# Three-step warm-up of a fused attention and channel-mix kernel: half projections, weight transposes and the order of step 2 moved

## The chip, the cores and the metric

The kernel runs on one core of one Trainium2 chip, with one launch. The metric is the device time in microseconds (us) of that launch. Before the change it was 272.54 us, the median of three runs (272.11 to 272.74).

## The reference, cut to what matters

The input x has 4 sequences of 1024 tokens with 256 channels, all in float32. Two sublayers run one after the other:

```python
def _L0_attn_ref(x, ...):            # called with layernorm(x)
    q = x @ Wq + bq                  # 16 heads of 16
    k = (x @ Wk + bk) @ Wc @ We      # 4 key/value heads of 16
    v = (x @ Wv + bv) @ Wc @ We
    qf, kf = elu(q) + 1, elu(k) + 1
    num = einsum(qf, cumsum(kf v^T)) # causal linear attention along the tokens
    den = einsum(qf, cumsum(kf)) + 1e-6
    y = x + (num / den) @ Wo + bo
    return layernorm(y) * gamma + beta

def _L0_ffn_ref(x, ...):             # called with layernorm(x)
    x_prev = x shifted by one token, zero first
    xr = mu_r * x + (1 - mu_r) * x_prev
    xk = mu_k * x + (1 - mu_k) * x_prev
    return sigmoid(xr @ W_r.T) * (relu(xk @ W_k.T)**2 @ W_v.T)

x = x + _L0_attn_ref(layernorm(x), ...)
x = x + _L0_ffn_ref(layernorm(x), ...)
```

## The kernel before, in words

The tokens are cut into 8 chunks of 128; a chunk is 128 tokens of all 4 sequences, so its tiles are 128x1024 or 2x128x512. Each engine has its own instruction list, written out by hand; semaphores tie them together, and an engine stops at the first wait that is not met, whatever stands behind it. `step(c)` (c = 0 to 6) works on up to four chunks at once: the front (transposes, keys, values, queries) of chunk n = c+1, the attention of chunk c (scores, mask, outputs, division), the output projection and the norms of chunk m = c-1, and the channel mix of chunk f = c-2. So steps 0 and 1 have no channel mix; step 2 is the first with all four. `finale` drains the last ones.

The parts that the change and the prediction touch:

- TensorE. `out_projection(m, i, bank)` (L520) is half i of chunk m's projection, 8 matmuls. `ffn_weight(i, bank)` (L601) turns one of the three FFN weights with 4 transposes. `keep_busy` (L597) issues matmuls whose results nobody reads. `scores(c, b)` (L482), `outputs(c, b)` (L500), `denominators(n)` (L465, waits for `prod`), `mix_r`, `mix_k`, `mix_v_parts` as named. `step` (L607), `first_full_step` (L644) and `middle_of_step` (L658) give the order.
- VectorE (DVE). `mask` (L1142), `divide` (L1154), `add_residual` (L1165: the sum of projection and residual, then row statistics), `norm_x` (L1068), `token_shift` (L1201), `centre` (L1175), `states` and `key_sums` (L1121, L1115), `second_residual` (L1186), `reciprocal` (L1128, L1130).
- ScalarE (ACT). Copies out of PSUM (L828), exponentials of the queries (L848, L850), `normalise_x` (L894), `normalise_y` (L900), `normalise_z` (L910).
- GpSimd (POOL). `add_bo` (L269), `add_beta` (L276), `denominator_terms` (L284, writes `prod`), `token_difference` (L292, writes `dz`), `first_norm`, `second_norm` and `norm_x` (L227 to L237), `finish` (L299). In steps from 2 on, POOL's list is: token difference, norm of x, `add_bo(n)`, `first_norm(m)`, `add_beta(n)`, `denominator_terms(n)`, `second_norm(m)`, `finish(f)`. `add_beta(n)` overwrites a buffer of which there are two, so it begins with this wait, and `prod` stands behind it:

```python
if n >= 2:
    pool.wait_ge(s_x2, 4 * n - 4)      # all four rows of second_residual(n - 2)
```

The PSUM banks are x0, x1, x2 (one each), ps_y (outputs) and z0 to z3 (scores, reciprocals).

## Time and profile before

| | |
|---|---|
| median of 3 runs | 272.54 us (272.11 to 272.74) |
| the profiled execution's own time | 272.06 us |
| its span in the profile | 270.3 us |
| PE busy | 258.1 us (95%) |
| DVE busy | 233.2 us (86%) |
| ACT busy | 168.8 us (62%) |
| POOL busy | 149.0 us (55%) |
| granted TensorE clock | 1.00 |

All times in the rows below are of the profiled execution, counted from the start of its span; 1.8 us of its own time lie outside the span. A row gives start and duration; the duration of a pipelined group is a little longer than the distance to the next one. An item in brackets behind a row is the idle time ahead of it and what ended it.

### The profile page before, as it was taken

Reading aid. Unit: us, or ns where it says so; the run is one execution under the profiler, and the core shown is the slowest. Engines: PE = TensorE matmul, PEld = TensorE weight load, DVE = VectorE, ACT = ScalarE, POOL = GpSimd, SP = SyncE. Lnnn points to the kernel's source line nnn. Section 1 sums busy time; section 2 is a strip of 40 time slices with the busy share of each in tenths; the row PEclk is TensorE's granted clock in tenths of the full one; section 3 lists DMA queues with packets and bytes.
Section 4 is the critical chain, followed back from the end, with each engine's and each line's share of the span. In section 5 each row is a group of like instructions: output and inputs, shape, how many; then the busy total and the mean of one; then the engine's idle time right before and its main releaser. Section 6 shows DMA issues by size and latency. Waiting matters only on the chain.

```text
span 270.3 us, 7775 instructions
## 1 busy us (share of the span) xinstructions
PE 258.1 (95%) x3047; PEld 195.4 (72%) x3047; DVE 233.2 (86%) x562; ACT 168.8 (62%) x339; POOL 149.0 (55%) x171
## 2 busy tenths in 40 slices
PE   7998989999998999999999999999999999999893
PEld 6867657877874788759875888758875877686663
DVE  6677779889799899998999899996999868999694
ACT  2579786794667856586648765686348730357570
POOL 3567484579944695366833685366433533173542
PEclk9999999999999999999999999999999999999999
DMA  6910320000200040002200020002000020000213
GB/s 180 266 67 4 79 80 2 4 2 0 81 2 0 2 158 0 2 4 76 82 2 0 2 81 1 2 4 78 2 0 4 2 80 2 0 0 0 80 42 116
DMA packets 12180, 10.75 MB, mean 40 GB/s; under 512 B 2288, under 2 KB 12144, under 8 KB 12144
## 3 DMA queue, kind: packets, MB, share of 16 engines
q1 hardware_dynamic: 11392, 9.97, 12.1%
q8 instruction: 24, 0.39, 0.6%
q10 hardware_dynamic: 752, 0.30, 0.5%
q14 instruction: 12, 0.10, 0.1%
HBM read 6.07 MB, written 4.19 MB: 38 GB/s over the span
## 4 chain that ended last, share of the span: by engine, by line
PE 52%; DVE 26%; ACT 9%; issue 6%; POOL 4%; DMA 2%; ACTq 0%; DVEq 0%; POOLq 0%
PE ps_x L539 7%; PE ps_x L524 7%; PE ps_x L546 5%; PE ps_z L495 5%; PE ps_x L428 4%; PE ps_x L577 4%; PE ps_y L511 4%; PE ps_y L516 4%; DVE xk L1201 4%; DVE stats L1068 3%; DVE probs L1142 3%; DVE qf L1106 2%; DVE xr L1201 2%; PE ps_x L532 2%; ACT eq L848 2%
## 5 line engine op out<-in xcount | busy, mean ns | idle before, releaser
L1142 DVE TENSOR_TENSOR probs<-ps_z,causal 128x1024 f32<-128x1024 f32 x32 | 38.7, 1209 | 2.6 <-PE ps_z L495 2.3
L276 POOL TENSOR_TENSOR xb_tok<-x_in,beta_bc 128x1024 f32<-128x1024 f32 x8 | 19.1, 2382 | 21.0 <-DVE x_tok L1186 21.0
L524 PE MATMUL ps_x<-wo_sb,oT 128*128 128x256 f32 x128 | 30.1, 383 | 0.0
L284 POOL TENSOR_TENSOR prod<-qf,ksum 128x1024 f32<-128x1024 f32 x7 | 16.6, 2365 | 24.1 <-DVE ksum L1115 24.1
L299 POOL TENSOR_TENSOR out_tok<-tanh_r,x_tok 128x512 f32<-128x512 f32 x14 | 18.3, 1314 | 19.6 <-DVE tanh_r L1213 19.3
L524 PEld LDWEIGHTS ps_x<-wo_sb,oT 128*128 128x128 f32 x128 | 23.4, 190 | 3.8 <-issue 0.5
L269 POOL TENSOR_TENSOR abo_tok<-a_tok,bo_bc 128x1024 f32<-128x1024 f32 x8 | 18.9, 2368 | 11.9 <-DVE kf L1100 3.5
L495 PE MATMUL ps_z<-qf,kfT 32*128 32x128 f32 x512 | 23.3, 296 | 1.6 <-ACT kfT L828 1.3
L229 POOL TENSOR_TENSOR rstd<-rstd,neg_half 128x4 f32<-128x4 f32 x22 | 23.0, 1046 | 1.7
L495 PEld LDWEIGHTS ps_z<-qf,kfT 32*128 32x128 f32 x512 | 17.2, 185 | 7.3 <-issue 3.6
L511 PE MATMUL ps_y<-qf,state 32*32 32x128 f32 x512 | 20.5, 274 | 1.0 <-DVE oT L1154 0.4
L516 PE MATMUL ps_y<-probs,v_pad 128*32 128x128 f32 x512 | 20.6, 279 | 0.0
L511 PEld LDWEIGHTS ps_y<-qf,state 32*32 32x32 f32 x512 | 11.9, 104 | 12.0 <-issue 8.6
L894 ACT ACTIVATE a_tok<-x_in,nbias,rstd 128x256 f32<-128x256 f32 x28 | 14.6, 589 | 8.9 <-issue 5.4
L539 PE MATMUL ps_x<-xk,wkT 128*128 128x512 f32 x40 | 18.5, 605 | 1.2 <-DVE qf L1106 0.9
L910 ACT ACTIVATE z_tok<-x_tok,nbias,rstd 128x256 f32<-128x256 f32 x32 | 16.7, 593 | 3.4 <-POOL nbias L237 2.2
L546 PE MATMUL ps_x<-wrT,xr 128*128 128x256 f32 x80 | 18.1, 379 | 0.0
L292 POOL TENSOR_TENSOR dz<-zT 128x512 f32<-128x512 f32 x14 | 14.5, 1059 | 5.5 <-ACT zT L828 5.4
L848 ACT ACTIVATE eq<-ps_x,neg_bq 128x512 f32<-128x512 f32 x15 | 10.2, 681 | 11.5 <-PE ps_x L444 11.4
L1106 DVE SCALAR_TENSOR_TENSOR qf<-ps_x,bq,eq 128x512 f32<-128x512 f32 x15 | 11.2, 746 | 6.5 <-ACT eq L850 6.5
L516 PEld LDWEIGHTS ps_y<-probs,v_pad 128*32 128x32 f32 x512 | 12.0, 109 | 6.3 <-issue 6.1
L1201 DVE SCALAR_TENSOR_TENSOR xr<-dz,mu_r_col,zT 128x512 f32<-128x512 f32 x16 | 14.1, 918 | 2.8 <-POOL dz L292 2.8
(194 smaller groups left out, 683.2 us busy)
## 6 DMA issues: line engine op xcount, KB each, us to landing
x_in<-in_L_attn_x_dram SPq DMA_DIRECT2D x8, 512.0 KB, 4.6
out_dram<-out_tok SPq DMA_DIRECT2D x16, 256.0 KB, 2.1
xr<-in_L_attn_Wq_dram ACTq DMA_DIRECT2D x1, 256.0 KB, 4.1
xk<-in_L_ffn_W_r_dram SPq DMA_DIRECT2D x1, 256.0 KB, 5.0
xk<-in_L_ffn_W_k_dram SPq DMA_DIRECT2D x1, 256.0 KB, 5.2
xr<-in_L_ffn_W_v_dram SPq DMA_DIRECT2D x1, 256.0 KB, 5.8
wo_sb<-in_L_attn_Wo_dram SPq DMA_DIRECT2D x4, 64.0 KB, 4.6
bo_bc<-in_L_attn_bo_dram SPq DMA_DIRECT2D x1, 128.0 KB, 5.0
```

The source lines that it names most:

```text
L229: PL.tensor_tensor(dst[:], dst[:], neg_half[:], ALU.pow).then_inc(done, 1)
L269: PL.tensor_tensor(abo_tok[n % 2][:], a_tok[n % 2][:], bo_bc[:].unsqueeze(1).to_broadcast([P, NB, D]), ALU.add).then_inc(s_ab, 1)
L276: PL.tensor_tensor(xb_tok[n % 2][:], x_in[n % XBUF][:], beta_bc[:].unsqueeze(1).to_broadcast([P, NB, D]), ALU.add).then_inc(s_xb, 1)
L299: PL.tensor_tensor(out_tok[:, 2 * i:2 * i + 2, :], tanh_r[:, i].rearrange("p (b d) -> p b d", b=2), x2_tok[m % 3][:, 2 * i:2 * i + 2, :], ...
L495: last = mm(ps_z[:, g, u * P:(u + 1) * P], kfT[c % 2][rows, 2 * b + u, :, :], qf[c % 2][rows, :, t0:t0 + HALF], start=True, stop=True, ski ...
L511: mm(ps_y[rows, off + u * P:off + (u + 1) * P], state[rows, slot, b, :, :], qf[c % 2][rows, :, t0:t0 + HALF], start=(u == 0), stop=False, ...
L516: last = mm(ps_y[32 * g:32 * g + 32, off + u * P:off + (u + 1) * P], v_pad[c % 2][:, b, u, g, :, :], probs[b % 2][:, g, u * P:(u + 1) * P] ...
L524: last = mm(bk_[:, (b % 2) * D:(b % 2 + 1) * D], oT[m % 2][:, a, b, :], wo_sb[:, a, :], start=(a == 0), stop=(a == 1))
L539: last = mm(bk_[:, :], wkT[:, k, n * P:(n + 1) * P], xk[:, k, :, :], start=(k == 0), stop=(k == KD - 1))
L546: last = mm(bk_[:, (b % 2) * D:(b % 2 + 1) * D], xr[:, k, b, :], wrT[:, k, :], start=(k == 0), stop=(k == KD - 1))
L1142: V.tensor_tensor(probs[b % 2][:].rearrange("p g (r s) -> p g r s", s=HALF), ps_z[:, :, 0:2 * P].rearrange("p g (r s) -> p g r s", s=HALF) ...
L1201: V.scalar_tensor_tensor(out=dst[:, k], in0=dz[:, k], scalar=mu[:, k:k + 1], in1=zT[:, k, :, 0:P], op0=ALU.mult, op1=ALU.add).then_inc(don ...
```

## The change

Six things change in the lists; the arithmetic stays.

1. The first half of the output projection of chunks 0 and 1, `out_projection(c, 0, x1)`, moves from the start of steps 1 and 2 to the tail of steps 0 and 1, before `scores(n, 0)`. In step 1 it takes the place of `keep_busy(8)`. Its residual sum on DVE moves along (`residual_sum(c, 0, x1)`, ahead of `mask(n, 0)`); the row statistics stay behind (`residual_stats`).
2. The FFN weights W_r and W_k are transposed in the prologue (`keep_busy(5)` instead of 10 beside them), with the copy of W_r on ACT between the query exponentials and the `kfT` copies. W_v is transposed early in step 0. The copies of W_v and W_k stand early in ACT's step 0.
3. ACT's step 1 copies the reciprocals ahead of `aT_high`; DVE's `low_a` in step 1 moves behind the keys.
4. Step 2 gets a list of its own on PE and DVE: z is transposed after the first outputs, r's mixing (`mix_r`) comes behind the queries, `scores(2, 3)` ahead of the state increments.
5. On DVE in step 2, `token_shift` for r comes after `mask(2, 2)`, and `centre` and `second_residual` come after the queries, `second_residual` behind `key_sums`.
6. On POOL in step 2, `add_bo(3)` comes first and `token_difference(0)` after the norm of x. On ACT in step 2, `normalise_x` and the tanh of r come after the queries.

```diff
             def step(c):
                 n, m, f = c + 1, c - 1, c - 2
-                if f >= 0:
+                if f == 0:
+                    add_bo(n)
+                if f >= 1:
                     token_difference(f)
                 if n + 1 < NC:
                     norm_x(n + 1)
                 if f >= 0:
-                    add_bo(n)
+                    if f == 0:
+                        token_difference(0)
+                    else:
+                        add_bo(n)
                     first_norm(m)
                     add_beta(n)
                     denominator_terms(n)
...
                 if f == 0:
                     first_full_step(c, n, m)
-                    return middle_of_step(c, n, m, f)
+                    return end_of_step(c, n, m, f)
                 if f >= 1:
                     pe.wait_ge(s_den, c + 1)
                     pe.wait_ge(s_gt, 2 * f - 1)
                     out_projection(m, 0, x1)
                 else:
                     transpose_a(n, 1, (s_den, c + 1))
-                    if m >= 0:
-                        pe.wait_ge(ffn_w_sb, 3)
-                        out_projection(m, 0, x1)
-                    else:
-                        pe.wait_ge(ffn_w_in, FFN_IN)
-                        pe.wait_ge(s_qf, 2)
-                        ffn_weight(0, x1)
+                    if m < 0:
+                        pe.wait_ge(ffn_w_sb, 1)
+                        ffn_weight(2, ps_y)
                     pe.wait_ge(s_pr, 8 * c + 2)
                     spread_reciprocals(c, (z0, z1, z2, z3))
                 if m >= 0:
                 else:
                     keys_values(n)
                     scores(c, 1)
+                    pe.wait_ge(ffn_w_sb, 2)
                 middle_of_step(c, n, m, f)
+                end_of_step(c, n, m, f)
 
             def first_full_step(c, n, m):
                 transpose_a(n, 0, (s_kT, 2 * c + 2))
                 transpose_a(n, 1, (s_den, c + 1))
-                out_projection(m, 0, x1)
-                pe.wait_ge(s_aT, 2 * n + 2)
-                transpose_z(0, x0, x2)
                 pe.wait_ge(s_pr, 8 * c + 2)
                 spread_reciprocals(c, (z0, z1, z2, z3))
                 pe.wait_ge(s_y, 2 * m + 1)
                 out_projection(m, 1, x1)
                 scores(c, 1)
+                keys_values(n)
+                outputs(c, 0)
+                pe.wait_ge(s_y, 2 * m + 2)
+                transpose_z(0, x2, x1)
+                scores(c, 2)
+                pe.wait_ge(s_kv, 2 * n + 2)
+                query_parts(n, 0, x0)
                 pe.wait_ge(s_zT, 2)
-                keys_values(n)
+                query_parts(n, 1, x1)
+                outputs(c, 1)
+                mix_r(0, 0, x2)
+                pe.wait_ge(s_qf, 2 * n + 1)
+                mix_r(0, 1, x0)
+                pe.wait_ge(s_th, 1)
 
             def middle_of_step(c, n, m, f):
...
+            def end_of_step(c, n, m, f):
                 keys_transposed(n)
-                state_increments(n)
-                scores(c, 3)
+                if f == 0:
+                    scores(c, 3)
+                    pe.wait_ge(s_th, 2)
+                    state_increments(n)
+                else:
+                    state_increments(n)
+                    scores(c, 3)
                 pe.wait_ge(s_qf, 2 * n + 2)
                 if f >= 0:
                     mix_k(f, 0, x1)
                     pe.wait_ge(s_tail, n + 1)
                     mix_k(f, 1, x0)
-                elif m < 0:
-                    ffn_weight(1, x1)
                 outputs(c, 2)
                 if f >= 0:
                     pe.wait_ge(s_rl, 2 * f + 2)
                 else:
                     pe.wait_ge(s_tail, n + 1)
-                    if m < 0:
-                        pe.wait_ge(ffn_w_sb, 2)
-                        ffn_weight(2, x1)
                 if f >= 0:
                     denominators(n)
                     outputs(c, 3)
                     mix_v_parts(f, 1, x2)
                     scores(n, 0)
                 else:
-                    if m >= 0:
-                        keep_busy(8, x1)
+                    out_projection(c, 0, x1)
                     scores(n, 0)
                     outputs(c, 3)
                     denominators(n)
...
             pe.wait_ge(s_kv, 2)
             state_increments(0)
-            keep_busy(10)
+            keep_busy(5)
+            pe.wait_ge(ffn_w_in, FFN_IN)
+            ffn_weight(0, ps_y)
+            pe.wait_ge(s_qf, 1)
+            ffn_weight(1, x1)
             scores(0, 0)
             pe.wait_ge(pool_const, 2)
...
-                if f == 0:
-                    normalise_z(0)
-                    shift_z(0, x0, x2)
                 if c == 0:
-                    act.wait_ge(ffn_w_ps, 1)
-                    copy(flat(wrT), x1[:, :]).then_inc(ffn_w_sb, 1)
-                if c in (0, 2):
+                    act.wait_ge(ffn_w_ps, 3)
+                    copy(flat(wvT), ps_y[:, :], scale=0.5).then_inc(ffn_w_sb, 1)
+                if c <= 2:
                     reciprocals(c)
                 for k in range(KD):
                     act.wait_ge(s_aT, 2 * n + k + 1)
                     copy(aT_p[0][:, k, :], aT[:, k, :]).then_inc(s_aTh, 1)
-                if c == 1:
-                    reciprocals(c)
+                if f == 0:
+                    normalise_z(0)
+                if f <= 0 and c != 1:
+                    keys(n)
                 if c == 0:
+                    copy(flat(wkT), x1[:, :]).then_inc(ffn_w_sb, 1)
+                if f == 0:
+                    shift_z(0, x2, x1)
+                elif n + 1 < NC:
+                    normalise_x(n + 1)
+                if c == 1 or f >= 1:
                     keys(n)
-                if n + 1 < NC:
-                    normalise_x(n + 1)
-                if c >= 1:
-                    keys(n)
-                if f >= 0:
+                if f >= 1:
                     gate_r(f, 0, x1)
                 if c == 1:
                     normalise_y(m)
                 if c == 0:
                     act.wait_ge(ffn_w_sb, 1)
                     copy(flat(wr_p[0]), flat(wrT)).then_inc(wr_split, 1)
-                if f >= 0:
+                if f >= 1:
                     gate_r(f, 1, x2)
                 queries(n, 0, x0)
                 queries(n, 1, x1)
+                if f == 0:
+                    normalise_x(n + 1)
+                    gate_r(0, 0, x2)
+                    gate_r(0, 1, x0)
                 values(n)
                 if c == 0:
-                    act.wait_ge(ffn_w_ps, 2)
-                    copy(flat(wkT), x1[:, :]).then_inc(ffn_w_sb, 1)
                     keys_transposed(n)
                 state_blocks(n)
...
             normalise_x(1, (2, 3))
             queries(0, 0, x1)
             queries(0, 1, z0)
+            act.wait_ge(ffn_w_ps, 1)
+            copy(flat(wrT), ps_y[:, :]).then_inc(ffn_w_sb, 1)
...
             def add_residual(m, i, bk_):
+                residual_sum(m, i, bk_)
+                residual_stats(m, i)
+
+            def residual_sum(m, i, bk_):
                 if i == 0:
                     dve.wait_ge(s_ab, m + 1)
                     if m >= 1:
                 dve.wait_ge(s_y_ps, 2 * m + i + 1)
                 V.tensor_tensor(y_tok[:, 2 * i:2 * i + 2, :], bk_[:, :].rearrange("p (b d) -> p b d", b=2),
                                 abo_tok[m % 2][:, 2 * i:2 * i + 2, :], ALU.add).then_inc(s_y, 1)
+
+            def residual_stats(m, i):
                 dve.wait_ge(s_y, 2 * m + i + 1)
...
+                if f == 0:
+                    residual_stats(m, 0)
                 if n + 1 < NC:
                     norm_x(n + 1)
                 if f < 0:
                     short_step(c, n, m)
                     return
                 if f == 0:
-                    add_residual(m, 0, x1)
+                    first_full_step(c, n, m)
+                    return
                 token_shift(f, 0, *for_r)
                 token_shift(f, 1, *for_r)
-                if f == 0:
-                    add_residual(m, 1, x1)
-                if f >= 1:
-                    add_residual(m, 0, x1)
-                    add_residual(m, 1, x2)
+                add_residual(m, 0, x1)
+                add_residual(m, 1, x2)
                 mask(c, 1)
                 keys_values(n)
                 centre(m)
...
             def short_step(c, n, m):
                 if m >= 0:
-                    low_a(n)
-                    add_residual(m, 0, x1)
+                    residual_stats(m, 0)
                     add_residual(m, 1, x2)
                     mask(c, 1)
                     keys_values(n)
+                    low_a(n)
...
                     second_stats(m, (2, 3))
+                residual_sum(c, 0, x1)
                 mask(n, 0)
                 reciprocal(n)
                 divide(c, 3)
+
+            def first_full_step(c, n, m):
+                mask(c, 1)
+                add_residual(m, 1, x1)
+                keys_values(n)
+                low_a(n)
+                key_features(n)
+                divide(c, 0)
+                mask(c, 2)
+                token_shift(0, 0, *for_r)
+                token_shift(0, 1, *for_r)
+                queries(n, 0, x0)
+                queries(n, 1, x1)
+                divide(c, 1)
+                token_shift(0, 0, *for_k)
+                token_shift(0, 1, *for_k)
+                centre(m)
+                states(n)
+                key_sums(n)
+                second_residual(m)
+                mask(c, 3)
+                second_stats(m)
+                divide(c, 2)
+                low_part(0, 0)
+                low_part(0, 1)
+                reciprocal(n)
+                divide(c, 3)
+                gate(0, 0, x1)
+                gate(0, 1, x2)
```

## Rows read from the trace of the kernel before

**Rows 1.** the page: busy time of each engine, and the granted clock in 40 slices.

```profile
PE 258.1 (95%) x3047; PEld 195.4 (72%) x3047; DVE 233.2 (86%) x562; ACT 168.8 (62%) x339; POOL 149.0 (55%) x171
...
PEclk9999999999999999999999999999999999999999
```

**Rows 2.** the view of windows: us, busy time of each engine, clock, DMA share, GB/s.

```profile
57.00:84.00 27.00, 26.14 (x364) 20.39 (x360) 25.02 (x63) 17.83 (x38) 20.18 (x19) 1.00 0.08 22
...
110.00:140.00 30.00, 29.82 (x368) 22.60 (x367) 27.77 (x68) 20.43 (x41) 17.41 (x17) 1.00 0.12 36
```

**Rows 3.** the timeline, prologue and start of step 0: start, us, engine, line, operation.

```profile
18.13 2.50 PE L599 MATMUL ps_z<-ident 128*128 128x128 f32 x20
...
19.65 1.26 ACT L828 ACTIVATE kfT<-ps_x,row_mask 128x512 f32<-128x512 f32 x2 [0.88 <-DVE ksum L1115]
...
23.91 0.60 PE L604 MATMUL ps_x<-ident,xk 128*128 128x128 f32 x4
...
24.67 0.59 ACT L828 ACTIVATE wrT<-ps_x 128x512 f32<-128x512 f32 x1
```

**Rows 4.** the timeline, step 0.

```profile
29.88 2.06 ACT L894 ACTIVATE a_tok<-x_in,nbias,rstd 128x256 f32<-128x256 f32 x4
...
35.28 0.75 DVE L1106 SCALAR_TENSOR_TENSOR qf<-ps_x,bq,eq 128x512 f32<-128x512 f32 x1 [0.49 <-ACT eq L850]
...
39.42 0.73 PE L495 MATMUL ps_z<-qf,kfT 32*128 32x128 f32 x16 [0.93 <-ACT kfT L828]
...
40.34 1.23 DVE L1142 TENSOR_TENSOR probs<-ps_z,causal 128x1024 f32<-128x1024 f32 x1 [0.82 <-PE ps_z L495]
...
41.10 0.62 PE L469 MATMUL ps_x<-prod,head_cols 128*32 128x128 f32 x16
```

**Rows 5.** the timeline, step 1 and the start of step 2.

```profile
42.69 1.89 PE L524 MATMUL ps_x<-wo_sb,oT 128*128 128x256 f32 x8
...
46.17 0.68 DVE L1165 TENSOR_TENSOR y_tok<-ps_x,abo_tok 128x512 f32<-128x512 f32 x1
...
47.77 2.08 ACT L894 ACTIVATE a_tok<-x_in,nbias,rstd 128x256 f32<-128x256 f32 x4 [1.44 <-POOL nbias L237]
...
53.84 0.67 ACT L848 ACTIVATE eq<-ps_x,neg_bq 128x512 f32<-128x512 f32 x1
...
58.88 2.05 PE L599 MATMUL ps_x<-ident 128*128 128x128 f32 x16
...
63.56 0.95 DVE L1130 RECIPROCAL rden<-rden 128x128 f32<-128x128 f32 x1
```

**Rows 6.** the timeline, step 2.

```profile
67.38 0.73 PE L478 MATMUL ps_z<-rden,head_rows 32*128 32x128 f32 x16
...
68.21 2.04 POOL L292 TENSOR_TENSOR dz<-zT 128x512 f32<-128x512 f32 x2
...
69.29 2.17 DVE L1201 SCALAR_TENSOR_TENSOR xr<-dz,mu_r_col,zT 128x512 f32<-128x512 f32 x2 [1.41 <-POOL dz L292]
...
69.96 0.73 PE L495 MATMUL ps_z<-qf,kfT 32*128 32x128 f32 x16
...
73.18 1.19 DVE L1142 TENSOR_TENSOR probs<-ps_z,causal 128x1024 f32<-128x1024 f32 x1
...
80.29 2.38 POOL L276 TENSOR_TENSOR xb_tok<-x_in,beta_bc 128x1024 f32<-128x1024 f32 x1 [3.37 <-DVE x_tok L1186]
...
84.60 3.70 PE L539 MATMUL ps_x<-xk,wkT 128*128 128x512 f32 x8 [0.94 <-DVE qf L1106]
...
86.66 2.38 POOL L284 TENSOR_TENSOR prod<-qf,ksum 128x1024 f32<-128x1024 f32 x1 [3.99 <-DVE ksum L1115]
...
89.99 0.64 PE L511 MATMUL ps_y<-qf,state 32*32 32x128 f32 x16
```

**Rows 7.** the view of windows, DVE from `mask(2, 1)` to the end of `key_sums(3)`.

```profile
73.18:86.58 13.40, 12.46 (x163) 8.79 (x162) 13.29 (x30) 9.13 (x21) 6.04 (x4) 1.00 0.01 1
```

**Rows 8.** the view of waits on PE over the whole span: us in total, times, longest.

```profile
PE ps_x L532 <- ACT z_tok L910: 1.1, 1, 1.1
```


## What the change does to the time, predicted before it ran

> **What bounds the kernel now.** I read the page first, for busy times and clock. PE is busy 95% of the span and its granted clock is full in all 40 slices [rows 1]. Then windows by stage: from 110 to 140 us PE is busy 29.82 of 30.00, so in the later steps only PE's work counts, and a delay at the end of step 2 is handed on to the end. In steps 1 and 2 (57 to 84) PE has 0.86 us idle and DVE 25.02 busy of 27.00, a stage that two engines share [rows 2]. Last the chain of waits and the timeline, to see which wait ends last in steps 0 to 2. So one question decides: when PE can start `outputs(2, 3)`, the last piece of step 2 that waited for anything, at 89.99 before [rows 6]. Behind it the lists of PE are as they were.
>
> I carry times along the trace; "now" is the time forecast for the changed kernel.
>
> **Prologue.** ACT ran the `kfT(0)` copies at 19.65 after 0.88 idle, released by `key_sums`. Now the W_r copy stands ahead of them and waits for its transposes. PE does the 10 remaining matmuls of the 20 from 18.13 (half of 2.50, so 19.38) and then 4 transposes (0.60): 19.98. The copy of 0.59 ends at 20.6, so `kfT` starts 0.95 late [rows 3]. Its reader is `scores(0, 0)`, then mask, denominators, reciprocals, keys, each waiting in turn, so I carry +0.95 through. The transposes of W_k cost nothing, PE would wait for `kfT`. W_v's transposes take the slot that W_r's had, and its copy the slot of the W_r copy.
>
> **Step 0.** ACT is back to back from `a_tok` at 29.88 to the second query exponential, which DVE waits for at 35.28 [rows 4]. The W_k copy now stands ahead of `a_tok`: +0.55 (row of 0.59, less the overlap). That makes +1.5 at `qf(1)`, and at `key_sums`, `kfT(1)` and `scores(1, 0)`, at which PE arrived 0.93 early [rows 4]. PE has two sets of transposes less there and one half projection more (8 matmuls, 1.89 [rows 5]): `outputs(0, 2)` at 37.95, projection to 40.85, `kfT` ready at 40.9. It fits. The residual sum (0.68) on DVE falls before `mask(1, 0)`, ahead of which DVE was idle 0.82 [rows 4, 5]. Both are free here. Were that cover gone, they would cost 1.7 and 0.65.
>
> **Step 1.** All starts 1.5 late, `denominators(1)` at 42.6 instead of 41.10 [rows 4]. PE no longer does the half projection at 42.69 (1.89, spacing 1.73), and the spread of the reciprocals, which stood behind it, waits only for the reciprocal at 44.6. So PE has 1.3 back and is 0.1 to 0.2 late. DVE no longer has one sum (0.68). But the norm of x(3) is still 1.5 late, `a_tok` starts at 49.3 instead of 47.77 [rows 5], and ACT, which was idle later in this step, follows with keys, `normalise_y` and the key copy: the query exponential at 54.2 instead of 53.84, +0.36. `keep_busy(8)` (2.05 [rows 5]) covered nothing but idle time, and the half projection in its place is about as long. At the end of step 1 DVE is full: the sum (0.65) now stands between the statistics of x2(0) and `mask(2, 0)`, where there were only some 0.3 us free. Reciprocal(2) then starts at 64.2 instead of 63.56: +0.65 [rows 5], bounds +0.3 (the sum hidden) and +1.0 (nothing hidden).
>
> **Step 2, PE.** Reciprocal ends 65.15. From the spread at 67.38 to `scores(2, 1)` at 69.96 took 2.58, with one half projection between, as now [rows 6]. So `scores(2, 1)` stands at 67.7: two to three us early, the gain of the change. A mask starts 0.92 after its scores (39.42 to 40.34 [rows 4]): `mask(2, 1)` at 68.6. DVE, with division, half statistics and the norm of x before it, is there at 68.0.
>
> **Step 2, DVE, the step that decides.** Before, from `mask(2, 1)` at 73.18 to the end of `key_sums(3)` at 86.58, DVE was busy 13.29 of 13.40 [rows 7]. This stretch held `second_residual(1)`. The new list has the same operations from `mask(2, 1)` to the end of `second_residual(1)`, only that it is now last, and besides, the two shifts for r and the second residual sum with statistics, which stood ahead: 73.18 - 69.29 = 3.89 [rows 6]. Together 17.29, so `second_residual(1)` ends at 68.6 + 17.3 = 85.9. The wait for `dz` comes on top: POOL starts `add_bo(3)` only once the second sum is done (70.1), takes 2.4 for it (as `add_beta`, same shape), 2.04 for `dz` [rows 6], and between them 1.7 to 2.6 for the small operations of the norm (an estimate: the reciprocal power of it alone has a mean of 1.05 on the page); `dz` is complete at 76.2 to 77.1, DVE wants it at 76.5. 0 to 0.6, I take 0.3. `second_residual(1)` ends at 86.2; it ended at about 80.2, where POOL's wait for it ended [rows 6].
>
> POOL's `add_beta(3)` waits for exactly that: it started at 80.29, after 3.37 idle, released by `x_tok` [rows 6]. Behind it in POOL's list stands `prod(3)`, which had started at 86.66 when `key_sums` was done. Now the two stand one after the other behind `second_residual`: 86.2 + 2.38 + 2.38 = 90.95. PE's `denominators(3)` waits for it. PE gets there sooner. From `scores(2, 1)` to `outputs(2, 3)` it took 20.03; now the z transposes come in (twice 0.5) and 0.94 idle [rows 7] and the denominators (0.5) go out: 67.7 + 19.6 = 87.3. **New stall** of 3.6 us. Then denominators (0.45 until the next, row of 0.62 [rows 4]) and `outputs(2, 3)` at 91.4 instead of 89.99: **+1.4**. `divide(2, 2)`, behind the second statistics, is done at 89.4 and not last.
>
> **Sum.** Front +0.65. From reciprocal(2) to `outputs(2, 3)` 26.2 us instead of 25.5: +0.75. Behind it z of chunk 1 (`second_norm`, then `normalise_z`) is ready about 95, PE wants it at 96.3: no more cost. Steps 3 to 6 and the finale hand 1.4 on. The profiled execution took 272.06 us (270.3 in its span), so 273.5; against the median of 272.54 that is 273.9.
>
> **Rule against the change.** All PE gaps in the trace of before are short, the longest behind the start 1.1 us [rows 8], and the granted clock never left 2.4 GHz [rows 1]; mine is 3.6. The Trainium skill (TensorE: Matmul & The Clock Gate, "HAM oscillation — how this bites in real kernels") says that an idle stretch between matmul bursts can take TensorE back to its lower clock, and what follows starts slow. No row of before shows the lower level, so no run here bears this out yet; by the rule the sum would be that of rival C, by the rows 273.9.
>
> **The rivals.**
>
> A, the front's delay is absorbed: the W_r copy does not reach `kfT(0)`, or ACT catches up in step 1, and only DVE's longer way counts: 1.4 - 0.65 = +0.75 at most, +0.2 if DVE never waits for `dz` and the shifts run closer together. The middle, +0.5, gives 273.0. For it: ACT idle in step 1 (1.44 ahead of `a_tok` [rows 5]). Against: that idle waited for the norm, which is late itself.
>
> B, **faster**: the stall at `denominators(3)` does not decide. Then `outputs(2, 3)` starts when `divide(2, 2)` is done, at 89.05 if `second_residual` ends 1.6 us earlier than I have it (84.3 or before: 84.3 + 4.76 = 89.05). That is -0.95, 271.6 us. It decides if DVE's 17.3 us come out at under 15.8, or `mask(2, 1)` starts by 67. For it: PE has 1.73 us of work less in step 2 and PE and DVE are both early at `mask(2, 1)` by 4.6. Against: DVE was busy 13.29 of 13.40 in the same operations [rows 7], there is no slack to squeeze.
>
> C, the clock falls in the new stall. What follows takes up to twice as long; as a price I take one such block, `mix_k` with 3.70 [rows 6], once more: 277.6. Against: whether 3.6 us is enough nothing here shows.
>
> D, DVE and POOL are slower side by side than I have them: shifts at 1.1 each beside POOL instead of 0.8, the sum in step 1 unhidden, a late `dz`. +2.8, 275.3.
>
> **How the numbers follow.** Chances: forecast 0.60, A 0.14, B 0.12, C 0.06, D 0.08. A change within 0.2% (0.54 us) is no change that a measurement of this kernel can tell. Forecast, C and D are slower: 0.74; A counts as the same: 0.14; B faster: 0.12. The forecast's own bounds are those of the front (-0.35, +0.35), of `dz` (-0.3, +0.3) and of the durations (0.3): 273.0 to 274.9. The range reaches down into A and up to D: 272.4 to 275.4; below it lies B (0.12), above it C and a little of D.
>
> **What the changed profile would show.** A gap on PE of 3 to 4 us before the `denominators` of step 2, ended by POOL `prod`; `xb_tok(3)` released by DVE `x_tok` near 86 and `prod` right behind it. `kfT(0)` near 20.6; `scores(2, 1)` near 67.7; `outputs(2, 3)` near 91.4; PE full behind. I am wrong if `prod(3)` is ready before PE is, if `scores(0, 0)` is not late, or if PE has new gaps in steps 3 to 6.

## The result: 4.8 us slower, and the profile after

The changed kernel took 277.19 us (276.66 to 277.66, 4 runs) against 272.4 for the kernel before, whose four runs here include the three behind the 272.54 above; the ratio of the two is 1.0174, 95% interval 1.0162 to 1.0187. The forecast was 273.9, range 272.4 to 275.4, so the direction was right and the size was not. The profiled execution took 276.66 us, its span is 274.9 (270.3 before). First the page of the kernel after, busy times and granted clock, as in [rows 1]:

```profile
PE 256.7 (93%) x3021; PEld 193.9 (71%) x3021; DVE 235.0 (85%) x562; ACT 168.8 (61%) x339; POOL 149.8 (54%) x171
...
PEclk9999999999999799999999999999999999999999
```

PE is busy 1.4 us less and the span is 4.6 longer, and one slice of the clock, the 14th (89.3 to 96.2 us), is no longer full. The waits on PE (us in total, times, longest) say where to look:

```profile
PE ps_x L474 <- POOL prod L284: 3.6, 1, 3.6
...
PE ps_z L500 <- ACT kfT L845: 1.4, 1, 1.4
...
PE ps_x L551 <- DVE xr L1227: 1.4, 1, 1.4
```

They are 3.6 us at the denominators, 1.4 for `kfT(0)` in the prologue and 1.4 for `xr` in step 2. The first and the last have no counterpart before; the waits for `kfT` came to 1.3 in two pieces there, the longer one 0.9. The timeline of the kernel after, in the order of the forecast's steps; the first fence answers to [rows 3] to [rows 5] and the start of step 2, the second to [rows 6]:

```profile
20.50 1.26 ACT L845 ACTIVATE kfT<-ps_x,row_mask 128x512 f32<-128x512 f32 x2
...
41.83 1.23 DVE L1162 TENSOR_TENSOR probs<-ps_z,causal 128x1024 f32<-128x1024 f32 x1
...
53.71 0.67 ACT L865 ACTIVATE eq<-ps_x,neg_bq 128x512 f32<-128x512 f32 x1
...
63.96 0.95 DVE L1150 RECIPROCAL rden<-rden 128x128 f32<-128x128 f32 x1
...
67.64 0.73 PE L500 MATMUL ps_z<-qf,kfT 32*128 32x128 f32 x16
...
68.56 1.23 DVE L1162 TENSOR_TENSOR probs<-ps_z,causal 128x1024 f32<-128x1024 f32 x1 [0.99 <-PE ps_z L500]
```

```profile
70.53 2.36 POOL L269 TENSOR_TENSOR abo_tok<-a_tok,bo_bc 128x1024 f32<-128x1024 f32 x1 [2.07 <-DVE y_tok L1189]
...
72.14 1.90 DVE L1290 TENSOR_TENSOR aT_low<-aT,aT_high 128x512 fp32r<-128x512 f32 x2
...
75.43 2.04 POOL L292 TENSOR_TENSOR dz<-zT 128x512 f32<-128x512 f32 x2
...
76.50 2.17 DVE L1227 SCALAR_TENSOR_TENSOR xr<-dz,mu_r_col,zT 128x512 f32<-128x512 f32 x2 [0.24 <-POOL dz L292]
...
78.73 3.72 PE L551 MATMUL ps_x<-wrT,xr 128*128 128x256 f32 x16 [1.38 <-DVE xr L1227]
...
84.01 0.29 DVE L1141 TENSOR_TENSOR tail<-ps_x,tail 128x128 f32<-128x128 f32 x1 [0.78 <-PE ps_x L466]
...
85.72 1.65 DVE L1212 SCALAR_TENSOR_TENSOR x_tok<-y_tok,rstd,xb_tok 128x256 f32<-128x256 f32 x4
...
87.45 2.37 POOL L276 TENSOR_TENSOR xb_tok<-x_in,beta_bc 128x1024 f32<-128x1024 f32 x1 [7.90 <-DVE x_tok L1212]
...
89.77 2.35 POOL L284 TENSOR_TENSOR prod<-qf,ksum 128x1024 f32<-128x1024 f32 x1
...
90.45 2.81 DVE L1296 TENSOR_TENSOR ka_low<-k_act,ka_high 128x512 fp32r<-128x512 f32 x2
...
92.26 0.64 PE L474 MATMUL ps_x<-prod,head_cols 128*32 128x128 f32 x16 [3.55 <-POOL prod L284]
...
92.84 0.64 PE L516 MATMUL ps_y<-qf,state 32*32 32x128 f32 x16
...
98.53 0.73 PE L500 MATMUL ps_z<-qf,kfT 32*128 32x128 f32 x16
```

Read it from the bottom. `scores(3, 0)` is the last row, and this is its row in the kernel before:

```profile
94.20 0.73 PE L495 MATMUL ps_z<-qf,kfT 32*128 32x128 f32 x16
```

It starts at 98.53, before at 94.20: +4.33 of the 4.6. Of these, `outputs(2, 3)` is 2.85 late (92.84, before 89.99 [rows 6]). From there to `scores(3, 0)` it takes 5.69 instead of 4.21: 1.48 more for the same matmuls. Above stand the causes: PE waits 3.55 for POOL's `prod`, `prod` stands behind `xb_tok` (`add_beta`), and that waited 7.90 for DVE's `x_tok`, which is `second_residual(1)`. The 1.48 is the clock, as the windows show (us, then busy time of PE, PEld, DVE, ACT, POOL, the clock, DMA share, GB/s):

```profile
88.00:92.00 4.00, 0.71 (x24) 0.38 (x16) 3.96 (x12) 2.71 (x5) 4.00 (x2) 1.00 0.00 0
...
93.00:94.00 1.00, 1.00 (x28) 0.77 (x24) 0.96 (x3) 0.00 (x0) 0.92 (x2) 0.72 0.06 16
...
94.00:95.00 1.00, 1.00 (x14) 0.62 (x7) 0.88 (x2) 0.27 (x1) 0.62 (x2) 0.50 0.00 0
...
96.00:97.00 1.00, 1.00 (x7) 1.00 (x6) 0.00 (x0) 0.91 (x3) 0.00 (x0) 0.58 0.00 0
...
97.00:98.00 1.00, 1.00 (x11) 1.00 (x10) 0.69 (x1) 0.00 (x0) 0.00 (x0) 1.00 0.00 0
```

PE is busy 0.71 of 4 us, and a little after it resumes its granted clock goes from 2.4 to 1.2 GHz and stays there for about three us.

### The profile page after: what moved, and what is told of

Its sections match the earlier page's. It is cut to its first block, busy times and chain, and to the rows that moved or that the text cites. A ratio compares the mean times of both kernels' runs of the same rounds, so it can differ in the third digit from the quotient of the medians.

```text
span 274.9 us, 7721 instructions
## 1 busy us (share of the span) xinstructions
PE 256.7 (93%) x3021; PEld 193.9 (71%) x3021; DVE 235.0 (85%) x562; ACT 168.8 (61%) x339; POOL 149.8 (54%) x171
## 4 chain that ended last, share of the span: by engine, by line
PE 55%; DVE 18%; POOL 9%; issue 8%; ACT 6%; DMA 2%; ACTq 0%; DVEq 0%; POOLq 0%
PE ps_x L529 9%; PE ps_x L544 5%; PE ps_x L551 5%; PE ps_z L500 5%; PE ps_x L433 4%; PE ps_x L582 4%; PE ps_y L521 4%; PE ps_y L516 4%; DVE xk L1227 3%; DVE probs L1162 3%; DVE stats L1088 2%; PE ps_z L483 2%; PE ps_x L537 2%; PE ps_x L586 2%; PE ps_x L426 2%
## 5 line engine op out<-in xcount | busy, mean ns | idle before, releaser
L551 PEld LDWEIGHTS ps_x<-wrT,xr 128*128 128x128 f32 x80 | 14.8, 190 | 3.5 <-DVE xr L1227 1.6
L433 PE MATMUL ps_x<-wkv_sb,aT 128*128 128x128 f32 x128 | 16.4, 281 | 0.0
```

Of the source, the lines that this page charges most:

```text
L433: last = mm(x0[:, b * P:(b + 1) * P], aT[:, k, b * P:(b + 1) * P], wkv_sb[:, k, :], start=(k == 0), stop=(k == KD - 1))
L551: last = mm(bk_[:, (b % 2) * D:(b % 2 + 1) * D], xr[:, k, b, :], wrT[:, k, :], start=(k == 0), stop=(k == KD - 1))
```

## The experiments

All times are medians, each ratio is to the kernel before, which ran at 272.2 to 272.3 beside them, and the brackets behind a ratio are its 95% interval. The edits of e1 to e6 and of e10 are shown against the changed kernel, that of e7 against the kernel before, that of e12 against e1, of e11 against e6, of e8 on top of e3 and e5, and of e9 against e8.

The prologue starts up to 0.6 us earlier or later from one traced execution to the next: the scan of the key sums in it begins at 18.21 in the kernel before, 18.23 in the changed one, 18.16 in e4 and 18.79 in e7. A start time of one trace set against that of another carries this difference; waits and durations do not.

**e1, `prod` ahead of `add_beta` in GpSimd's step 2.**

```diff
-                    add_beta(n)
                     denominator_terms(n)
+                    add_beta(n)      # f == 0 only
```

> The changed kernel (277.2 us), with prod(3) ahead of add_beta(3) in GpSimd's list in step 2. My theory: prod(3) starts when key_sums is done (85.8 instead of 89.8) and TensorE's wait of 3.55 us at the denominators goes. The next wait is outputs(2, 3) for divide(2, 2), which is done at 90.5, so outputs(2, 3) starts at 90.6 instead of 92.84 (-2.2), and the granted clock does not fall (-1.5): 273.5 us. Rival, VectorE's longer way alone is the cost and the order on GpSimd only moves the wait: outputs(2, 3) stays near 92.5 and the time above 276.5.

Measured: 277.84 us, ratio 1.021 (1.0193 to 1.0228), worse than the change itself. My number missed by 4.3. The rival's numbers came (`outputs(2, 3)` late, above 276.5), but for another reason than it gave. The stall moved from the denominators to `outputs(2, 3)`; the timeline of e1 shows why:

```profile
85.96 3.76 DVE L1216 SCALAR_TENSOR_TENSOR x_tok<-y_tok,rstd,xb_tok 128x256 f32<-128x256 f32 x4
...
86.12 2.52 POOL L284 TENSOR_TENSOR prod<-qf,ksum 128x1024 f32<-128x1024 f32 x1 [6.34 <-DVE ksum L1139]
...
92.49 0.39 DVE L1178 TENSOR_TENSOR oT<-ps_y,rden_bc 128x256 f32<-128x256 f32 x1
...
92.94 1.08 PE L520 MATMUL ps_y<-qf,state 32*32 32x128 f32 x16 [3.51 <-DVE oT L1178]
```

One line of its windows shows the clock (the last number but two):

```profile
91.00:92.00 1.00, 0.00 (x0) 0.00 (x0) 1.00 (x4) 0.01 (x1) 1.00 (x1) 0.73 0.00 0
```

`second_residual(1)`, four instructions that took 1.65 us together, took 3.76 beside `prod`. Everything on DVE behind it slipped, `divide(2, 2)` with it, PE stood 3.51 us, and the clock fell all the same (0.988 in all four runs), here while PE was still waiting. Why it was slow beside `prod` was open; e12 settles it.

**e12, e1 with DVE waiting until `prod` is done.**

```diff
+                dve.wait_ge(s_prod, 4)
                 second_residual(m)
```

> e1 (277.84: prod(3) ahead of add_beta(3) on GpSimd, second_residual(1) took 3.76 us instead of 1.66), with one wait more: VectorE starts second_residual(1) only when prod(3) is done. Theory, the two share a way to SBUF and second_residual was held up by prod: started at 88.7 it takes 1.66 again and ends at 90.4 instead of 89.7, so the time is at most 0.7 more, 277.8 to 278.5. Rival, second_residual is slower in this order for another reason: 3.76 us again, the time 2.5 more, 280.3.

Measured: 277.55 us (2 runs). The timeline of e12:

```profile
86.30 2.35 POOL L284 TENSOR_TENSOR prod<-qf,ksum 128x1024 f32<-128x1024 f32 x1 [6.34 <-DVE ksum L1139]
...
88.68 1.67 DVE L1216 SCALAR_TENSOR_TENSOR x_tok<-y_tok,rstd,xb_tok 128x256 f32<-128x256 f32 x4 [2.46 <-POOL prod L284]
```

1.67 us again when it runs alone, so the rival is out. DVE waited 2.46 us and still ended `second_residual` only 0.6 later than in e1 (90.35 against 89.72, of which 0.2 is the start of the prologue): beside `prod` it had hardly got on. `prod` itself took 2.35 alone and 2.52 beside it. So it is VectorE that is shut out here, and GpSimd loses little. With two runs against four, 277.55 and 277.84 cannot be told apart. The Trainium skill (SBUF — State Buffer, "Who interferes with whom") has the rule: VectorE with two inputs in SBUF contends with a GpSimd instruction that reads SBUF; the traces agree, with 3.76 against 1.67.

**e4, `second_residual(1)` ahead of `states(3)` and `key_sums(3)`.**

```diff
                 centre(m)
+                second_residual(m)
                 states(n)
                 key_sums(n)
-                second_residual(m)
                 mask(c, 3)
```

> The changed kernel, with VectorE's second_residual(1) ahead of states(3) and key_sums(3) in step 2. GpSimd's order stays. Theory: second_residual ends at 85.0 to 85.6 instead of 87.4, add_beta and prod follow at once, prod(3) is done at 90.2 instead of 92.1; the wait on TensorE is 1.8 us, too short for the clock to fall; outputs(2, 3) at 90.9: 277.2 - 1.9 - 1.5 = 273.8 us. Rival, the chain through prod does not set the end: no change. If the clock falls all the same, 275.3.

Measured: 272.56 us (10 runs), ratio 1.0012 (1.0002 to 1.0021), clock 1.00 in eight runs, 0.998 and 0.997 in the other two. One line moved up by two places gives back 4.6 of 4.8 us. The timeline of e4:

```profile
85.02 2.36 POOL L276 TENSOR_TENSOR xb_tok<-x_in,beta_bc 128x1024 f32<-128x1024 f32 x1 [5.36 <-DVE x_tok L1212]
...
87.33 2.37 POOL L284 TENSOR_TENSOR prod<-qf,ksum 128x1024 f32<-128x1024 f32 x1
...
89.85 0.64 PE L474 MATMUL ps_x<-prod,head_cols 128*32 128x128 f32 x16 [1.02 <-POOL prod L284]
...
90.43 0.64 PE L516 MATMUL ps_y<-qf,state 32*32 32x128 f32 x16
...
94.64 0.73 PE L500 MATMUL ps_z<-qf,kfT 32*128 32x128 f32 x16
```

The wait for `prod` is 1.02 us, `outputs(2, 3)` starts 0.44 later than before, and from there to `scores(3, 0)` it takes 4.21. It gave 1.2 us more than I had written: `second_residual` also fills the 0.78 us in which DVE had waited ahead of `states(3)`. That a wait of 1.8 us would be too short for the clock to fall was a guess; the wait came out at 1.02, and in e6 below the clock fell behind one of 1.32. `prod` now ends (89.70) before DVE's `ka_low` starts, which took 1.28, against 2.81 in the changed kernel, where it ran beside `prod`.

**e2, the stall kept, PE kept busy in it.**

```diff
                     pe.wait_ge(s_rl, 2 * f + 2)
+                    keep_busy(12, x1)      # f == 0 only
```

> The changed kernel, with 12 matmuls that nobody reads issued by TensorE in its wait ahead of denominators(3) of step 2 (12 by 0.25 = 3.0 us of the 3.55). The wait stays, only TensorE is not idle in it. Theory: the clock falls because TensorE stands idle, so it stays at 2.4 GHz here, outputs(2, 3) to scores(3, 0) takes 4.2 us as in the kernel before instead of 5.7: 275.6 us. Rival, the clock falls for another reason or costs nothing that shows at the end: 277 us, clock below 1.00.

Measured: 275.16 us, ratio 1.011 (1.0095 to 1.0125), 2.0 less than the changed kernel. Timeline of e2:

```profile
89.02 2.94 PE L604 MATMUL ps_x<-ident 128*128 128x128 f32 x24
...
92.56 0.65 PE L474 MATMUL ps_x<-prod,head_cols 128*32 128x128 f32 x16 [0.60 <-POOL prod L284]
...
93.14 0.64 PE L516 MATMUL ps_y<-qf,state 32*32 32x128 f32 x16
...
97.35 0.73 PE L500 MATMUL ps_z<-qf,kfT 32*128 32x128 f32 x16
```

`outputs(2, 3)` to `scores(3, 0)` is 4.21 again with 2.94 us of unread matmuls in the wait. The denominators are no earlier. So the loss has two parts: 2.8 to 3.0 us of lateness (2.85 at `outputs(2, 3)`, 3.0 by the median of e2), and for the clock 1.5 in the profiled execution, the fastest of the four and the one with the highest clock (0.993), and 2.0 by the medians (0.986 to 0.991 in the others).

**e7, the kernel before, with `second_residual(1)` behind `key_sums(3)` as its only edit.**

```diff
                 low_a(n)
-                second_residual(m)
+                if f != 0:
+                    second_residual(m)
...
                 key_sums(n)
+                if f == 0:
+                    second_residual(m)
```

> The kernel before (272.2 us) with one edit: in step 2, second_residual(1) behind key_sums(3) on VectorE. Theory: it ends at 86.6 instead of 80.2, add_beta and prod end at 91.4 instead of 89.0, TensorE is at the denominators at 87.6 and stands idle 3.7 us: outputs(2, 3) +1.9 and the granted clock falls (+1.5): 274.1 if the clock holds, 275.6 if it falls. Rival, the place of second_residual alone costs nothing in the old order: 272.2.

Measured: 276.68 us, ratio 1.0164 (1.0147 to 1.0181): with front, projections and the rest of step 2 as before, this place alone makes nearly all of the loss. The wait on PE in e7:

```profile
PE ps_x L469 <- POOL prod L284: 3.6, 1, 3.6
```

The row of `add_beta(3)` in its timeline:

```profile
87.93 2.36 POOL L276 TENSOR_TENSOR xb_tok<-x_in,beta_bc 128x1024 f32<-128x1024 f32 x1 [10.41 <-DVE x_tok L1186]
```

The same 3.6 us, and a lower clock in every run (0.987 to 0.991). `xb_tok` starts at 87.93; less the 0.6 by which this trace starts late that is 87.3, where I had 86.6. The time missed my 275.6 by 1.1.

**e3, the copy of W_r behind the `kfT(0)` copies.**

```diff
-            act.wait_ge(ffn_w_ps, 1)
-            copy(flat(wrT), ps_y[:, :]).then_inc(ffn_w_sb, 1)
...                                   # the two kfT copies
+            act.wait_ge(ffn_w_ps, 1)
+            copy(flat(wrT), ps_y[:, :]).then_inc(ffn_w_sb, 1)
```

> The changed kernel, with ScalarE's copy of W_r in the prologue behind the two kfT(0) copies instead of ahead of them. Theory: scores(0, 0) starts at 21.0 instead of 21.8, and of these 0.85 us what steps 0 and 1 had not absorbed comes back: the reciprocal of step 1 was 0.40 late, so 0.4 to 0.8 less, 276.6 us. Rival, the delay is absorbed before step 2: within 0.2 of 277.2. Other rival, a copy later in ScalarE's list delays step 0 as much: no change either, but with state and v_pad 0.6 late.

Measured: 276.58 us, ratio 1.0163 (1.0146 to 1.018), 0.6 less than the changed kernel, and e10 below shows the same 0.6 against e4. The delay that the copy of W_r makes reaches the end.

**e6, the changed front with the old step 2**, all four lists of step 2 as before, less the half projection. Of its diff, the start of PE's list:

```diff
                 transpose_a(n, 1, (s_den, c + 1))
+                pe.wait_ge(s_aT, 2 * n + 2)
+                transpose_z(0, x0, x2)
                 pe.wait_ge(s_pr, 8 * c + 2)
                 spread_reciprocals(c, (z0, z1, z2, z3))
...
```

> The changed kernel with the whole of step 2 (all four lists) put back to the order of the kernel before; prologue, step 0, step 1 and the moved half projections stay changed. Theory: the front hands step 2 a reciprocal 0.4 late (63.96 instead of 63.56); the half projection that is gone from the start of step 2 (1.73 us of TensorE) brings little, since there xr waits for GpSimd's dz behind add_bo(2) and add_beta(2): 272.4 to 272.9 us, 0 to +0.4. Rival, the moved projections by themselves are the gain that the new step 2 gave away: 271 us or less. Other rival, the front is most of the loss: 275 or more.

Measured: 273.91 us, ratio 1.0063 (1.0042 to 1.0083), and a wide spread over 7 runs: 272.55 at clock 1.00, four from 273.67 to 274.26 at 0.994, 274.55 at 0.985 and 275.07 at 0.986. Only the run at full clock lies in my 272.4 to 272.9. The wait in e6 and its windows:

```profile
66.39 2.07 PE L532 MATMUL ps_x<-ident,z_tok 128*128 128x128 f32 x8 [1.32 <-ACT z_tok L908]
```

```profile
57.00:65.00 8.00, 7.31 (x143) 5.32 (x131) 7.92 (x21) 4.46 (x11) 5.83 (x8) 1.00 0.01 2
...
65.00:66.00 1.00, 0.06 (x1) 0.00 (x0) 1.00 (x4) 0.84 (x2) 1.00 (x1) 1.00 0.00 0
...
68.00:70.00 2.00, 2.00 (x19) 1.45 (x19) 0.00 (x0) 1.39 (x3) 1.80 (x2) 0.50 0.03 10
...
72.00:74.00 2.00, 2.00 (x16) 1.26 (x18) 0.88 (x2) 0.22 (x1) 1.54 (x3) 0.50 0.03 9
```

In the profiled run, the slowest of the seven, PE had one wait of 1.32 us for `z_tok`, transposes about it, and then fell to 1.2 GHz for over six us.

**e11, e6 with PE kept busy in that wait.**

```diff
+                pe.wait_ge(s_y, 2 * m + 1)
+                keep_busy(5, x1)
                 pe.wait_ge(s_aT, 2 * n + 2)
                 transpose_z(0, x0, x2)
```

> The kernel with the old step 2 and the changed front (median 273.91, runs from 272.55 at clock 1.00 to 275.07 at 0.986), with 5 unread matmuls (1.25 us) in TensorE's wait for z_tok at the start of step 2. Theory: the spread of its runs is the clock, which falls in that wait of 1.3 us in most runs; kept busy, the clock stays at 1.00 in all runs and the time is 272.6, the front's own cost of 0.4. Rival, the clock falls for what stands before (the waits from 56 to 60), and the spread stays.

Measured: 272.69 us, 272.49 to 273.16 in 10 runs, ratio 1.001 (1.0001 to 1.002); clock 1.00 in seven runs, not under 0.997 in the others. So the front, moved half projections included, costs 0.4. The 1.73 us of PE time that leaves step 2 are not seen at the end: most of them became a wait for `z_tok`, in which 1.25 us of unread matmuls find room. The rival, that the waits before bring the clock down by themselves, is out, since they are the same here.

**e5, both edits of e1 and e4.**

```diff
-                    add_beta(n)
                     denominator_terms(n)
+                    add_beta(n)      # f == 0 only
...
+                second_residual(m)
                 states(n)
                 key_sums(n)
-                second_residual(m)
```

> The changed kernel with both edits of the last round: second_residual(1) ahead of states(3) and key_sums(3) on VectorE (that alone ran 272.56), and prod(3) ahead of add_beta(3) on GpSimd (that alone ran 277.84, with second_residual at 3.76 us instead of 1.66 while prod ran beside it). Theory: prod ahead of add_beta was slower only because GpSimd's prod and VectorE's second_residual, both with two inputs in SBUF, ran at the same time and VectorE had to wait. Here second_residual is done at 85.0, before prod can start (86.7): it takes 1.66 again, prod is done at 89.0, the denominators wait under 0.4, outputs(2, 3) at 90.0, clock 1.00: 272.1 us. Rival, prod ahead of add_beta is slow by itself (its place in GpSimd's list delays second_norm and z): 273 us or more.

Measured: 273.37 us, ratio 1.0041 (1.0027 to 1.0054), missed by 1.3 and 0.8 worse than e4. The rival's number came (273 or more), but not by `second_norm`. `second_residual` ran alone as said, and `outputs(2, 3)` started at 90.02 as I had it; but now `add_beta` had come to stand beside `ka_low` (`low_part`). Timeline of e5:

```profile
89.21 2.37 POOL L276 TENSOR_TENSOR xb_tok<-x_in,beta_bc 128x1024 f32<-128x1024 f32 x1
...
89.87 2.86 DVE L1300 TENSOR_TENSOR ka_low<-k_act,ka_high 128x512 fp32r<-128x512 f32 x2
...
92.79 0.50 PE L590 MATMUL ps_x<-wv_high,ka_low 128*128 128x256 f32 x2 [0.90 <-DVE ka_low L1300]
```

**e8, e5 with the copy of e3, the norm of x(4) ahead of `add_bo(3)` on GpSimd and `divide(2, 2)` ahead of the second statistics.** Beside the edits of e3 and e5:

```diff
-                if f == 0:
-                    add_bo(n)
...
                     norm_x(n + 1)
+                if f == 0:
+                    add_bo(n)
...
-                second_stats(m)
                 divide(c, 2)
+                second_stats(m)
```

> A repaired version of the changed kernel: the two edits of e5, the W_r copy behind kfT(0), on GpSimd in step 2 the norm of x(4) ahead of add_bo(3) so that dz starts when zT is ready (73.9 instead of 75.4), and divide(2, 2) ahead of the second statistics. Theory: front -0.6, xr complete near 77.2 instead of 78.7, the wait for prod gone, outputs(2, 3) at 88.6 to 89.2 instead of 89.99 in the kernel before: 270.9 to 271.5 us. Rival, DVE stays the bound from mask(2, 1) on and prod near 89: 272.0. Other rival, z of chunk 1 comes late behind add_beta and gives the gain back in step 3: 272.2 with a wait for z_tok.

Measured: 272.93 us, ratio 1.0028 (1.0017 to 1.004). Missed by 1.4. `outputs(2, 3)` did start earlier, at 89.34, but then PE waits 0.94 for `ka_low` as in e5.

**e9, the same with `add_beta` ahead of `prod` again.**

```diff
+                    add_beta(n)
                     denominator_terms(n)
-                    add_beta(n)
```

> The changed kernel with second_residual(1) ahead of states(3) (alone 272.56), the W_r copy behind kfT(0), the norm of x(4) ahead of add_bo(3) on GpSimd and divide(2, 2) ahead of the second statistics. add_beta stays ahead of prod. Theory: front -0.5, dz and with it xr 0.7 earlier, add_beta (84.3) and prod beside VectorE operations with one input in SBUF only, so nothing is slowed: outputs(2, 3) at 89.2 to 89.5 instead of 90.4, 271.5 us. Rival, GpSimd's next instructions collide with VectorE's two-input ones elsewhere: 272.5 as e4.

Measured: 272.58 us, ratio 1.0012 (1.0003 to 1.0021). The rival was right; against e10 below (271.92) these two further edits on GpSimd and VectorE cost 0.7 together. Timeline of e9:

```profile
71.70 1.90 DVE L1290 TENSOR_TENSOR aT_low<-aT,aT_high 128x512 fp32r<-128x512 f32 x2
...
73.05 2.50 POOL L292 TENSOR_TENSOR dz<-zT 128x512 f32<-128x512 f32 x2 [0.60 <-ACT zT L845]
...
73.53 1.13 DVE L1117 TENSOR_SCALAR ek<-ek 128x256 f32<-128x256 f32 x1
...
74.77 1.06 DVE L1120 SCALAR_TENSOR_TENSOR kf<-kb,ek 128x256 f32<-128x256 f32 x1
```

`dz` started 2.4 us earlier, and ran into `low_a` and the key features: `ek` 1.13 instead of 0.28, `kf` 1.06 instead of 0.43. `dz` itself took 2.50 instead of 2.04. `ek` has only one input in SBUF, so my assumption that such operations are safe beside GpSimd does not hold for it. PE's wait for `xr` shrank by 0.14 only.

**e10, e4 and e3 together.**

```diff
+                second_residual(m)
                 states(n)
                 key_sums(n)
-                second_residual(m)
...
-            act.wait_ge(ffn_w_ps, 1)      # ahead of the kfT(0) copies
-            copy(flat(wrT), ps_y[:, :]).then_inc(ffn_w_sb, 1)
...
+            act.wait_ge(ffn_w_ps, 1)      # behind them
+            copy(flat(wrT), ps_y[:, :]).then_inc(ffn_w_sb, 1)
```

> The changed kernel with second_residual(1) ahead of states(3), and the W_r copy of the prologue behind kfT(0). Theory: the two act in a row on one chain: 272.56 less the 0.6 that the copy gave alone = 272.0. Rival, with the stall gone the front is hidden behind GpSimd's chain: 272.5.

Measured: 271.92 us (271.78 to 272.28, 11 runs), ratio 0.9983 (0.9974 to 0.9992). This one beats both kernels, the one before by 0.4 us. The forecast was 272.0.

## Why the prediction was wrong, step by step

- Prologue: `kfT(0)` forecast at 20.6, measured 20.50. Right, and e3 shows that it counts.
- Step 0: the mask of `scores(1, 0)` 1.49 late, forecast 1.5. The half projection and the sum cost nothing. Right.
- Step 1: query exponential forecast 54.2, measured 53.71, reciprocal(2) forecast 64.2, measured 63.96: too high by 0.25 in this trace, which is the exception. Counted from the scan of the key sums in the prologue, reciprocal(2) is 0.38 late in it, but 0.58 to 0.60 late in all seven other traces with the same front (e1, e2, e4, e5, e6, e11, e12); forecast 0.65. One term on the way was wrong at no cost: I had the norm of x(3) 1.5 late, and `a_tok` was only 0.76 late, since GpSimd's small operations of that norm took 1.7 us instead of 2.5 once `low_a` no longer ran beside them.
- Step 2 to `mask(2, 1)`: forecast 68.6, measured 68.56. Right.
- **The first step that failed**, the term of 17.3 + 0.3 us for DVE from `mask(2, 1)` to the end of `second_residual(1)`. Measured: 68.56 to 87.37, 18.8, so 1.2 more than the 17.6. Two things were missing. `low_a` took 1.90 instead of 1.28: its first instruction (72.14) met the end of `add_bo(3)` (70.53 to 72.89) and took 1.30, the second 0.68. POOL's small operations are not the cause; beside them `low_a` took 1.26 in step 1 of the kernel before. This is the mechanism of rival D. And DVE stood 0.78 us ahead of `states(3)`: `xr` was complete at 78.67, PE waited 1.38 for it where I had counted an idle 0.94 as gone, and so the state increments came late. A list of operations that was full in one order was taken as full in the other, with the old prices.
- The chain behind it, `add_beta`, then `prod`, then the denominators, and a new stall of 3.6 us: measured 3.55. The mechanism was right, and e7 and e4 show it from both sides. That the size agrees so well is luck: `prod` ended 1.2 late (92.12, forecast 90.95) and PE stood at the denominators 1.4 late (88.7, forecast 87.3), and the two cancel in the wait, not in the time. `outputs(2, 3)` at 92.84, forecast 91.4.
- **The second step that failed**, the sum: it let the clock stand at no cost beside its own stall of 3.6 us, and gave rival C 0.06. The price of C (3.7) was too high, the real one was 1.5 to 2.0; its mechanism came in every run of the changed kernel (clock 0.986 to 0.993). The Trainium skill (TensorE: Matmul & The Clock Gate, "HAM oscillation — how this bites in real kernels") says that a long wait between bursts of matmuls takes TensorE back to its lower clock and that the next burst starts cold. The traces agree that it falls (0.50 behind a wait of 3.55), but not that the start is always cold: in the trace of after the clock was still 1.00 in the first us of new work. The longest gap in the trace of before (1.1 us [rows 8]) could not speak against a fall, and I let it.
- Behind `scores(3, 0)` 0.27 us more came up to the end, which I have not traced.

Together: 1.45 us too little before `outputs(2, 3)` and 1.5 to 2.0 too little behind it make up the 3.4 between 1.4 and 4.8. Of the rivals, A is out by e3, where taking away the front's delay gives 0.6 back. B is out by the trace of after: `divide(2, 2)` was done at 90.5, and `outputs(2, 3)` waited until 92.84 behind the stall. C came at about half its price, and D in the 0.6 of `low_a`.

What stays open: what exactly brought the clock down in e6, with a wait of 1.3 us, where the kernel before has a wait of 1.1 us and e4 one of 1.4 (for `xr`), and both hold 1.00 in their profiled runs. The length of one gap alone can't be it; keeping PE busy there was enough (e11).

## What to carry to other kernels

When an operation moves behind others in one engine's list, look for who waits for it on other engines, and what stands behind that wait there: here four 0.4 us instructions, moved back on VectorE, put two 2.4 us GpSimd operations on the path of TensorE. Price a stall on TensorE with the clock it may cost, and not by its length. And before two lists are put together anew, check which GpSimd operations that read SBUF come to lie beside VectorE operations with two SBUF inputs; here VectorE stood still for most of the time in which both wanted to run. e9 adds that one SBUF input (`ek`) is no safeguard.

## What the runs showed of the hardware that I had not expected

- VectorE with both inputs in SBUF makes next to no headway beside a large GpSimd operation: 3.76 instead of 1.66 for `second_residual`, 2.81 and 2.86 instead of 1.28 for `ka_low`. The GpSimd operation lost 0.17 (`prod` in e1) to 0.46 (`dz` in e9). An earlier GpSimd operation can so be a slower kernel (e1 against the changed kernel, e5 against e4; e9 against e10, where `divide(2, 2)` moved too).
- With 3.5 to 3.6 us of idle TensorE the fall of the clock did not come at a fixed place: about one us into the new work in the trace of after, about when it began in e7, and still in the wait in e1. It lasted some three us in the first two and over six in e1 and e6.
- TensorE's clock can fall in some executions of a kernel and hold in others: e6 ran from 272.55 to 275.07 with one program.
